# A gather moved out of the lookup by matmul, and another order of the second stage, in a DLRM tower on one core

## The reference

```
gram = einsum('bfd,bgd->bfg', all_emb, all_emb)      # 27 x 27 products of features
z    = gram[:, upper triangle]                        # 351 values
h    = concat(z, bottom)                              # 479
h    = relu(h @ W_top1 + b_top1)                      # 512
h    = relu(h @ W_top2 + b_top2)                      # 256
y    = h @ W_top3                                     # 1
```

## Time and profile before

| | |
|---|---|
| median of 3 runs | 103.09 us (102.77 to 103.11) |
| profiled execution, its own time | 102.85 us |
| its span | 101.1 us |
| PE busy | 96.3 us, 95% |
| PE weight loads busy | 82.5 us, 82% |
| DVE busy | 66.7 us, 66% |
| ACT busy | 57.7 us, 57% |
| POOL busy | 59.5 us, 59% |
| granted TensorE clock | 1.0 |

### The profile page before, as it was taken

One profiled execution on the slowest core, in us unless ns is written; L12 is line 12 of the kernel. 1 busy time (PEld: TensorE's weight loads), 2 busy tenths in 40 slices (PEclk: granted clock), 3 DMA queues, 4 the chain that ended last, 5 costly groups with the idle time before them and its releaser, 6 DMA issues.

```text
span 101.1 us, 3568 instructions
## 1 busy us (share of the span) xinstructions
PE 96.3 (95%) x1511; PEld 82.5 (82%) x1511; DVE 66.7 (66%) x164; ACT 57.7 (57%) x96; POOL 59.5 (59%) x63
## 2 busy tenths in 40 slices
PE   3999999999999999999999988999999999999992
PEld 3786777888888888888989777889989988899980
DVE  2499999999999999999797007503820483078001
ACT  5455949957997999993944303171343444412341
POOL 2677877778877877778777777777777100000000
PEclk9999999999999999999999999999999999999999
DMA  2989999999999999779821222222222100000000
GB/s 54 263 224 259 205 231 270 265 286 251 227 249 226 238 236 248 188 175 275 278 59 44 62 57 55 65 54 63 58 52 60 36 0 6 0 6 0 7 0 0
DMA packets 6512, 13.48 MB, mean 133 GB/s; under 512 B 2060, under 2 KB 2844, under 8 KB 6496
## 3 DMA queue, kind: packets, MB, share of 16 engines
q1 hardware_dynamic: 4536, 9.51, 37.1%
q0 software_dynamic: 1792, 3.67, 14.3%
q10 hardware_dynamic: 168, 0.07, 0.3%
HBM read 13.23 MB, written 0.01 MB: 131 GB/s over the span
## 4 chain that ended last, share of the span: by engine, by line
PE 90%; DVE 4%; ACT 2%; issue 2%; POOL 1%; POOLq 0%; ACTq 0%
PE acc L643 37%; PE acc L709 12%; PE acc L743 12%; PE acc L671 8%; PE ring L683 6%; PE ring L754 5%; PE acc L734 4%; DVE onehot L527 3%; PE acc L601 2%; PE ring L717 2%; PE ring L767 1%; PE acc L615 1%; ACT far L376 1%; PE ring L778 1%; ACT emb L441 1%
## 5 line engine op out<-in xcount | busy, mean ns | idle before, releaser
L345 POOL DMA_INDIRECT rows<-tbl,ids_sb x56 | 58.8, 1050 | 18.4 <-issue 16.8
L527 DVE TENSOR_SCALAR onehot<-far 125x512 fp32r<-125x512 f32 (+1 forms) x92 | 32.4, 411 | 1.5 <-ACT far L376 1.3
L643 PE MATMUL acc<-onehot,hi 125*128 125x512 f32 x84 | 24.0, 409 | 0.1
L643 PE MATMUL acc<-onehot,lo 125*128 125x512 f32 x84 | 22.4, 390 | 0.0
L643 PEld LDWEIGHTS acc<-onehot,hi 125*128 125x128 f32 x84 | 15.4, 193 | 4.1 <-DVE onehot L527 1.1
L643 PEld LDWEIGHTS acc<-onehot,lo 125*128 125x128 f32 x84 | 15.8, 188 | 3.4
L513 DVE TENSOR_TENSOR lo<-raw,hi 125x512 fp32r<-125x512 f32 (+1 forms) x24 | 16.8, 701 | 0.7 <-ACT hi L362 0.7
L548 DVE COPY gram<-acc 128x432 f32<-128x432 f32 x4 | 3.7, 918 | 20.1 <-PE acc L709 20.1
L362 ACT CAST hi<-raw 125x1024 fp32r<-125x1024 f32 (+1 forms) x11 | 12.0, 1086 | 7.8 <-PE acc L643 2.9
L709 PE MATMUL acc<-emb 128*27 128x27 f32 x1024 | 12.8, 192 | 1.2 <-issue 0.5
L709 PEld LDWEIGHTS acc<-emb 128*27 128x27 f32 x1024 | 10.8, 104 | 3.8 <-issue 1.8
(11 more groups left out here) (52 smaller groups left out, 84.1 us busy)
## 6 DMA issues: line engine op xcount, KB each, us to landing
raw<-tbl SPq DMA_DIRECT2D x9, 448.0 KB
raw<-tbl SPq DMA_DIRECT2D x2, 560.0 KB
ids_b<-ids SPq DMA_DIRECT2D x4, 256.0 KB, 7.4
rows<-tbl,ids_sb POOLq DMA_INDIRECT x56, 5.6
w1z<-w SPq DMA_DIRECT2D x3, 234.0 KB
w_sb<-w SPq DMA_DIRECT2D x1, 512.0 KB
raw<-tbl SPq DMA_DIRECT2D x9, 52.0 KB
raw<-tbl SPq DMA_DIRECT2D x2, 224.0 KB
```

Of the source, the lines that this page charges most:

```text
L345: nc.gpsimd.indirect_dma_start(out=rows[:, t, slot, :], out_offset=None, in_=tables[table], in_offset=bass.IndirectOffsetOnAxis(ap=ids_sb[ ...
L527: ins = nc.vector.tensor_scalar(onehot[:, n % OH_RING, k, of], far[:, t % FAR_RING, of], float(c), None, ALU.is_equal)
L643: mm = nc.tensor.matmul(acc[:, look_bank(t), :], part_of[:, t % HL_RING, c * D:(c + 1) * D], onehot[:, n % OH_RING, k, :], start=(half == ...
```

## The change

Table 1 (j = 0) is looked up for tiles 0 to 2 only, 384 of the 512 samples. For tile 3 its rows are gathered: `group(3, 3)` has three slots in place of two, so POOL issues a 57th transfer, after all others, and `turn 3 3` transposes and copies three. The two tables of the first pair (j = 0, 1) are now copied to `emb` by two instructions, one for three tiles of both and one for tile 3 of j = 1. The order of the tail is another.

```diff
+FIRST_TILES = 3
+def group(t, g):
+    slots = GROUPS[g]
+    return range(slots[0], NG + 1) if g == TURNS - 1 and t >= FIRST_TILES else slots
+def looked_up(j):
+    return FIRST_TILES * LANES if j == 0 else B
...
-              ("part", NL - 2, 0), ("part", NL - 2, 1), ("part", NL - 1, 0), ("part", NL - 1, 1), ("turn", 1, 2),
-              ("gram", 0, (0, 8)), ("bottom", 0, 0), ("turn", 1, 3), ("turn", 2, 0), ("part", NL - 2, 2),
-              ("gram", 0, (8, 20)), ("part", NL - 2, 3), ("part", NL - 1, 2), ("gram", 0, (20, 32)),
-              ("part", NL - 1, 3), ("turn", 2, 1), ("gram", 1, (0, 4)), ("bottom", 0, 1), ("gram", 1, (4, 12)),
-              ("turn", 2, 2), ("pairs", 0, 0), ("gram", 1, (12, 16)), ("bottom", 1, 0), ("l1", 0, 0), ("turn", 2, 3),
-              ("gram", 1, (16, 32)), ("l1", 0, 1), ("l1", 0, 2), ("l1", 0, 3), ("gram", 2, (0, 12)), ("turn", 3, 0),
-              ("l2", 0, 0), ("pairs", 1, 0), ("gram", 2, (12, 24)), ("l1", 1, 0), ("bottom", 1, 1), ("l1", 1, 1),
-              ("turn", 3, 1), ("gram", 2, (24, 32)), ("l1", 1, 2), ("l1", 1, 3), ("turn", 3, 2), ("l2", 1, 0),
-              ("turn", 3, 3), ("bottom", 2, 0), ("pairs", 2, 0), ("gram", 3, (0, 20)), ("bottom", 2, 1), ("l1", 2, 0),
-              ("l1", 2, 1), ("gram", 3, (20, 32)), ("l1", 2, 2), ("l1", 2, 3), ("l2", 2, 0), ("bottom", 3, 0),
-              ("pairs", 3, 0), ("bottom", 3, 1), ("columns", 0, 0), ("l1", 3, 0), ("l1", 3, 1), ("l1", 3, 2),
-              ("l1", 3, 3), ("l2", 3, 0), ("l2", 3, 1), ("l3", 3, 0)]
+              ("part", NL - 2, 0), ("part", NL - 2, 1), ("part", NL - 1, 0), ("part", NL - 1, 1), ("gram", 0, (0, 8)),
+              ("turn", 1, 2), ("bottom", 0, 0), ("part", NL - 2, 2), ("gram", 0, (8, 20)), ("turn", 1, 3),
+              ("bottom", 0, 1), ("part", NL - 2, 3), ("part", NL - 1, 2), ("gram", 0, (20, 32)), ("turn", 2, 0),
+              ("part", NL - 1, 3), ("turn", 2, 1), ("gram", 1, (0, 16)), ("bottom", 1, 0), ("pairs", 0, 0),
+              ("turn", 2, 2), ("l1", 0, 0), ("turn", 2, 3), ("gram", 1, (16, 32)), ("l1", 0, 1), ("l1", 0, 2),
+              ("l1", 0, 3), ("bottom", 1, 1), ("gram", 2, (0, 8)), ("turn", 3, 0), ("l2", 0, 0), ("pairs", 1, 0),
+              ("gram", 2, (8, 24)), ("l1", 1, 0), ("turn", 3, 1), ("bottom", 2, 0), ("l1", 1, 1), ("l1", 1, 2),
+              ("gram", 2, (24, 32)), ("bottom", 2, 1), ("turn", 3, 2), ("l1", 1, 3), ("l2", 1, 0), ("turn", 3, 3),
+              ("bottom", 3, 0), ("pairs", 2, 0), ("gram", 3, (0, 16)), ("l1", 2, 0), ("l1", 2, 1),
+              ("gram", 3, (16, 32)), ("l1", 2, 2), ("l1", 2, 3), ("l2", 2, 0), ("pairs", 3, 0), ("bottom", 3, 1),
+              ("columns", 0, 0), ("l1", 3, 0), ("l1", 3, 1), ("l1", 3, 2), ("l1", 3, 3), ("l2", 3, 0), ("l2", 3, 1),
+              ("l3", 3, 0)]
...
-                    of = acc[0:KP, spread_bank(j), :]
+                    of = acc[0:KP, spread_bank(j), 0:looked_up(j)]
...
-                        nc.scalar.copy(emb[:, :, :, first:first + 2],
-                                       acc[:, b:b + 2, :].rearrange("d j (t p) -> d t p j", t=TILES)
-                                       ).then_inc(emb_look, 2)
+                        tiles = FIRST_TILES if t == 1 else TILES
+                        nc.scalar.copy(emb[:, 0:tiles, :, first:first + 2],
+                                       acc[:, b:b + 2, 0:tiles * LANES].rearrange("d j (t p) -> d t p j", t=tiles)
+                                       ).then_inc(emb_look, 1 if t == 1 else 2)
+                        if t == 1:
+                            nc.scalar.copy(emb[:, tiles:, :, first + 1],
+                                           acc[:, b + 1, tiles * LANES:].rearrange("d (t p) -> d t p", p=LANES)
+                                           ).then_inc(emb_look, 1)
...
-                            of = slice(0, B if t < NL - 2 else PART)
+                            of = slice(0, looked_up(t) if t < NL - 2 else PART)
...
-                                mm = nc.tensor.matmul(acc[:, look_bank(t), :], part_of[:, t % HL_RING, c * D:(c + 1) * D],
-                                                      onehot[:, n % OH_RING, k, :],
+                                mm = nc.tensor.matmul(acc[:, look_bank(t), 0:looked_up(t)], part_of[:, t % HL_RING, c * D:(c + 1) * D],
+                                                      onehot[:, n % OH_RING, k, 0:looked_up(t)],
```

More of the change, by code:

```diff
@@ L200, in tower @@
         bot = sb("bot", [128, B])
-        rows = sb("rows", [128, TILES, NG, D])
+        rows = sb("rows", [128, TILES, NG + 1, D])
         emb = sb("emb", [128, TILES, LANES, FP])
@@ L340, in _ @@
             for t in range(TILES):
-                for g, slots in enumerate(GROUPS):
-                    for slot in slots:
-                        table = GATHERED[slot]
+                for g in range(TURNS):
+                    for slot in group(t, g):
+                        table = (GATHERED + LOOKED_UP)[slot]
                         col = t * TABLES + table
@@ L375, in difference @@
                 c = base_column(j)
-                nc.scalar.activation(far[:, j % FAR_RING, :], of, ACT.Identity,
+                nc.scalar.activation(far[:, j % FAR_RING, 0:looked_up(j)], of, ACT.Identity,
                                      bias=neg_row[:, c:c + 1]).then_inc(far_ready, 1)
@@ L446, in _ @@
                     b = bank(step, t, part)
-                    slots = GROUPS[part]
+                    slots = group(t, part)
                     n = len(slots)
@@ L614, in _ @@
                     for n in range(FIRST):
-                        nc.tensor.matmul(acc[:, spread_bank(n), :], pick[:, n:n + 1].broadcast_to([128, 128]), idt[:],
-                                         start=True, stop=True).then_inc(ids_spread, 1)
+                        nc.tensor.matmul(acc[:, spread_bank(n), 0:looked_up(n)], pick[:, n:n + 1].broadcast_to([128, 128]),
+                                         idt[:, 0:looked_up(n)], start=True, stop=True).then_inc(ids_spread, 1)
                     warm(WARM_ON)
```

## The result

The changed kernel takes 105.19 us (median of 4 runs, 104.63 to 105.63), the kernel before 102.93 us on the same chip (4 runs, 102.66 to 103.11): a ratio of 1.0229, 95% interval 1.0173 to 1.0284. That is 2.3 us slower. I had forecast 103.6 us within 102.6 to 104.2, so the way was right and the size wrong by a factor of more than four (0.5 us forecast). None of these eight runs is one of the slower executions, over 1.5% above a kernel's fastest, that some of the later sets hold.

A forecast was written before the change was run, and what follows sets the result against it. PE was taken as the bound (busy 95%, 90% of the chain), with early waits on DVE, ACT and a transfer. Terms summed to +0.50 us: 103.35 for the profiled execution, 103.6 as median, range 102.6 to 104.2.

The forecast's parts named there:

- Fewer pieces of grams: Second stage: 12 gram pieces become 10, saving small-to-large matmul changes, -0.40 us; bounds nothing and 0.8.
- the transpose: In turn 3 3: a third transpose is added work of PE, +0.11 us.
- the wait for `zt`: At the first l1, behind gram 1 (0, 16): PE waits for ACT's cut and copy, +0.10 us; bounds 0 and 0.3.
- the rival of the longer grams: Gram pieces of 16 steps run at the long piece's faster rate, saving 1.7 us: 102.3 us; chance 0.16.
- My sign of being wrong: Forecast wrong if 16-step gram pieces take 1.2 us, not 1.4 to 1.5, or look 1 keeps its distance from look 0.
- The wait before `gram 0`: gram 0 can't start earlier, PE idles 0.6 us, and turn 1 2 is done behind it: +0.44 us.
- The end: After gram 3: bottom 3 0 moved ahead delays the gram's end 0.45, pairs 3 gains at most 0.10: +0.35 us.
- The lookup: First stage: three tiles of j = 0 save little, as the landing of j = 1 binds: -0.10 us; bounds nothing and 0.92.
- The rival of the saving that arrives: First stage: rows of j = 1 land earlier and DVE's 0.75 us reaches PE: 102.9 us; chance 0.18.
- The rival of more waits than I counted: Second stage: l1 0 0 waits the full 0.3, fewer pieces give nothing: +1.1, 104.2 us; chance 0.13.

The follow-up runs named there:

- e2_lookup: The changed kernel with the old order of the tail put back, so only the lookup change: 102.32 us, ratio 0.9979 against the kernel before.
- e12_lookup: The lookup change alone with the old order once more, with more rounds: 102.93 us, ratio 0.9973 against the kernel before.
- e15_lookup_shift4: The lookup change alone with the old order, plus 4 matmuls of one column ahead of look 1: 102.52 us, ratio 0.9975 against the kernel before.
- e8_actload: The lookup change alone with the old order, rows of j = 1 issued by ACT instead of SP: 105.17 us, ratio 1.0200 against the kernel before.
- the shift of 20: 20 matmuls of one column ahead of look 1: 112.76 us, ratio 1.0944, on the changed kernel; 108.21 us, 1.0527, on the kernel before.
- e1_after: The changed kernel again, no edit: 104.73 us, ratio 1.0212 against the kernel before.
- e3_order: The kernel before with only the new order of the tail, all of table 1 looked up: 105.19 us, ratio 1.0219 against the kernel before.
- e5_bottom: The changed kernel with bottom 3 0 put back between l2 2 and pairs 3: 105.53 us, ratio 1.0292 against the kernel before.
- e6_turn: The changed kernel with turn 1 2 put back before gram 0: 104.89 us, no ratio to be had.
- e13_shift4: The changed kernel with 4 matmuls of one column ahead of look 1: 103.75 us, ratio 1.0143 against the kernel before.
- e14_shift10: The changed kernel with 10 matmuls of one column ahead of look 1: 105.42 us, ratio 1.0233 against the kernel before.
- e9_few_before: The kernel before with a quarter of the gram instructions, one matmul with weights of four samples in place of four: median 114.45 us.

## Why the prediction was wrong

**The step that failed** is "Fewer pieces of grams", -0.40. It took having two pieces fewer as a plain gain and put the grams' own length down as unchanged; but a gram is the one step whose length depends on where and in how long a piece it stands. The part that I had priced, the cost of going from a gram to a large matmul, seems to have been saved: between the grams, the steps that I can name in the changed kernel cost 0.50 (`turn 1 2` behind the wait), 0.44 (`bottom 3 0`), 0.11 (the transpose) and 0.40 (the wait for `zt`), 1.45 us, and the stretch outside the grams grew by only 0.88, so 0.57 went. The grams took most of it back, or more. In the kernel before they take 12.70 us from start to next, and in the other profiles of the old order 12.82, 11.83, 12.52 and 12.83 (`e2_lookup`, `e12_lookup`, `e15_lookup_shift4`, `e8_actload`), 12.5 in the mean. In those of the new order, without the shift of 20, they take 13.15, 13.01, 14.17, 12.71, 14.22, 12.67 and 12.92 (changed, `e1_after`, `e3_order`, `e5_bottom`, `e6_turn`, `e13_shift4`, `e14_shift10`), 13.3 in the mean. So the term that I put at -0.40 was, by the first two profiles, -0.57 + 0.45 = -0.12, and with the order alone about +1.0 (1.47 in the grams, and 0.90 outside them where the same steps without the transpose make some 1.4). I had seen the stops of 0.24 and 0.30 us in the timeline before, and noted for the rival of the longer grams that the spread of their rates might come from the steps around them; I did not price it.

Two things make the grams longer. One is the stops: in the order alone 0.44 and 0.81 us, against 0.24, 0.30 and 0.07 before, which is 0.6 of the 1.47. The other is pieces that are slower with no stop of over 0.1 us in them. The first 16 steps of `gram 1` take 1.37 to 1.61 us in three pieces, in the five profiles of the old order, and 1.72 to 1.90 as one piece in the seven of the new; pieces of 16 steps in `gram 1` and `gram 2` take 1.7 to 1.9 us everywhere, and the first of `gram 3` takes 1.20. My sign of being wrong, pieces of 16 steps at 1.2 us, came true for that one, and the others took 1.7 to 2.0, more than my 1.4 to 1.5. What slows them I can't say.

**What a stop is.** The page has a queue of 12 packets, 0.20 MB, kind "instruction":

```profile
q8 instruction: 12, 0.20, 0.8%
```

0.20 MB in 12 packets are 16 KB each. The trace has the start of each packet, and each longer stop ends a nearly constant time behind one:

```
kernel                 packet starts   PE goes on   between
before                     53.96         56.27        2.31
before                     57.90         60.12        2.22
changed                    54.10         56.37        2.27
changed                    87.45         89.87        2.42
order alone                53.58         56.23        2.65
order alone                87.72         90.44        2.72
changed, 20 matmuls        69.58         71.89        2.31
changed, 20 matmuls        95.48         97.82        2.34
before, 20 matmuls         87.16         89.86        2.70
```

I read this as PE having run out of program and waiting for its next block (the expectations call it a page); no view says so by name. For it speak the fixed places, the distance of 126 to 128 matmuls with as many weight loads, some 256 instructions, from one to the next, and the packet ahead of each. While PE computes large matmuls, a block lasts long enough that the next is there. A gram of 32 steps has 256 records that PE gets through in 2.4 us (128 in 1.20 in `gram 3` of the changed kernel), which is two blocks in about the time that one takes to come; if it meets a block's end soon after the next was asked for, it stands. The Trainium skill, "Runtime: NRT & Kernel Launch", section "Instruction fetch mechanics", says that instructions come in 16 KiB blocks of 256, and that the cost of crossing a block is mostly hidden. The size agrees with the 16 KB per packet and the distance between the stops; "mostly hidden" doesn't hold in the grams of this kernel, where crossings cost up to 2.33 us. With fewer instructions the stops are gone and the 12 packets become 6, and a shift moves the stops to other steps, while the 1350th record stays their place.

**The other terms.** The wait before `gram 0`: +0.44, measured 0.50, and right. (The parts took 0.11 longer besides, 4.87 us up to `gram 0` against 4.76, for which I had no term.) The wait for `zt`: +0.10, measured 0.40, over my upper bound of 0.3. From the end of the gram's piece to the first `l1` it is 1.71 us where I had 1.6 (ACT begins its cut 0.42 us behind PE), and the three steps that PE has meanwhile take 1.31 and not 1.5. The end: I had +0.45 - 0.10, and got 0.45; from the end of `gram 3` to the last `l1` it is 4.79 us in both, with `pairs 3` 3.61 behind the gram's end in both, so the 0.10 did not come. The transpose: 0.11, right. The lookup: the mechanism held, and the size hangs on the landing. With three tiles the first turn starts 9.24 to 9.26 us behind the landing of j = 1 (9.13 and 18.37; 8.29 and 17.55; 8.24 and 17.48), with all tiles at 18.05 and 18.02 for landings at 8.66 and 8.22, so there it does not follow the landing. The lookup gives 0.5 us with a landing at 8.3, and with one at 9.1 the first turn is 0.3 later than in the profile before; my -0.10 is for the landing of the one profile that I had. The rival of the saving that arrives had the mechanism and too large a price: 0.5 us with the earliest landings, and not 0.75. The rival of more waits than I counted, +1.1, came nearest to the outcome, with more of the wait for `zt` and pieces that give nothing, but without longer grams. The rival that longer grams run faster had the sign wrong for all pieces but one. (Of its "five new pieces of 16 steps" one, `gram 1 (16, 32)`, was there before.)

**The sum made again.** Terms from the first two profiles: lookup and landing +0.34, parts +0.11, grams +0.45, between them +0.88, end 0: +1.8 us, which is what the spans show. Against my +0.50 that is 0.44 more at the lookup, 0.30 at the wait for `zt`, 0.28 at the pieces, 0.11 in the parts, 0.10 at the end and 0.06 before `gram 0`. The 0.44 is the landing, which came early again in the next profile, so it is mostly chance and no loss of the change. The medians differ by 2.26, and the order alone, with no late landing, reaches as much (2.3 in its span) by grams that are 1.47 longer and 0.90 between them. Which executions have the longer grams, only the profiled ones show. The runs spread over about 2 us for the changed kernel (103.68 to 105.90) and for the kernel before beside it (101.73 to 103.70) alike.

**What stays open.** I can't say from these traces what makes PE ask for a block when it does; in the profiles the packet starts between 0 and some 130 records before the end of the block at hand. Nor what slows the long pieces of `gram 1` and `gram 2`, or why the grams of one kernel differ by 1 us (12.82 and 11.83 in the two profiles of the lookup alone). So which shift is a good one can't be computed here, only tried.

No version came out that is clearly faster than both. The lookup alone, at 0.9979 and 0.9973, is not shown to be faster than the kernel before, and is some 2% faster than the changed one; if a part of this change is kept, it is that.

## What to carry to other kernels

A stage of very short matmuls can be bound by the supply of its program as well as by the array. Look in the timeline for idle time of PE put down to "issue" and count the records up to it; if the count is the same in a variant with other steps there, it is a place in the program. Then an order must be judged by what stands around each such place, and one run of one order proves little. Do not price a step by one length: take its length from pieces of the size, and at the place, that the new order has. A step moved into another step's wait is worth what it covers there, and moving it out costs that, whatever else the order gains. And work saved ahead of a transfer is only worth as much as the transfer is early: issuing it sooner took the bandwidth here from the rows that were needed first.

## What I had not expected of the hardware

Twenty matmuls of one column, 1.1 us of work, made 8 us on the changed kernel and 5 on the one before. And a matmul with 108 columns of weights and 27 moving ones takes 0.186 us, while four with 27 and 27 together take 0.075: the short moving side didn't help here, where the weights are wide. In the kernels with these wide matmuls the granted clock fell to 0.5, the 1.2 GHz level, for some stretches (`e9_few_before`, tenths of full speed in 40 slices of the span):

```profile
PEclk9999999999999999999999955555999999999999
```
